# Interaction stage of a four-layer graph network: the order of VectorE's step, the add of a pair's sums moved to third place

## The reference

```
p1    = tanh(h @ pp_W1 + pp_b1) @ pp_W2 + pp_b2
inter = concat(p1[src], p1[dst]) @ pi_W1 + pi_b1
inter = (inter @ pi_W2 + pi_b2) @ pi_W3            # E x (64*8)
i1    = einsum('ecb,eb->ec', inter.reshape(E, 64, 8), edge_attr_8)
i1    = tanh(i1 @ ii_W1 + ii_b1) @ ii_W2 + ii_b2
out   = segment_sum(i1, dst)
```

## Time and profile before

| | before |
|---|---|
| median of 3 runs | 10613.77 us (10609.83 to 10619.3) |
| profiled execution | 10609.71 us, span 10608.1 us |
| PE, DVE, ACT, POOL busy | 56%, 41%, 23%, 65% of the span |
| gathers of the interaction stage | 1664, first start 4054.9 us, last 6334.5 us |

### The profile page before, as it was taken

How to read it: one execution, slowest core, us unless ns; L and a number is a source line. 1 busy time by engine, 2 the same in 40 slices (tenths; PEclk the granted TensorE clock), 3 DMA queues, 4 the chain that set the end, 5 groups by cost and what they waited for, 6 DMA issues and landing times.

```text
span 10608.1 us, 144590 instructions
## 1 busy us (share of the span) xinstructions
PE 5928.7 (56%) x31865; PEld 3642.0 (34%) x32026; DVE 4356.3 (41%) x11981; ACT 2422.2 (23%) x4618; POOL 6911.9 (65%) x7936
## 2 busy tenths in 40 slices
PE   6999997344444447888888882343333322222222
PEld 4777773222222223333333331232223211111111
DVE  5888884222322224666666662111111111111111
ACT  4999992000000002333333330000000000000000
POOL 2333330577777776766666666777777767777777
PEclk9999995555555558999999995555555555555555
DMA  3333332111111112222222221111111111111111
GB/s 96 97 97 97 97 96 79 48 29 30 29 30 29 30 30 48 57 56 56 56 56 56 56 51 23 28 28 28 28 28 28 28 24 28 28 28 28 28 28 27
DMA packets 503888, 488.54 MB, mean 46 GB/s; under 512 B 245340, under 2 KB 299425, under 8 KB 503777
## 3 DMA queue, kind: packets, MB, share of 16 engines
q0 software_dynamic: 220480, 235.58, 11.8%
q1 hardware_dynamic: 283360, 252.43, 8.2%
HBM read 427.04 MB, written 61.15 MB: 46 GB/s over the span
## 4 chain that ended last, share of the span: by engine, by line
POOL 43%; PE 25%; issue 19%; DVE 8%; DVEq 2%; POOLq 1%; ACT 1%; DMA 0%; another core or an unknown queue 0%; ACTq 0%; SPq 0%
POOL mov L668 43%; PE ps L1524 5%; PE ps L1413 4%; PE ps L1387 3%; PE ps L1420 3%; DVE scr L937 3%; PE ps L1516 2%; PE ps L1449 2%; PE ps L1543 1%; DVE sel L927 1%; PE ps L1411 1%; PE ps L1534 1%; DVE acc L946 1%; PE ps L1427 1%; PE ps L1428 0%
## 5 line engine op out<-in xcount | busy, mean ns | idle before, releaser
L1387 PE MATMUL ps<-outs,mov 128*64 128x64 f32 x9984 | 1371.0, 319 | 4210.3 <-DMA mov<-tab_q,idx 1613.2
L1387 PEld LDWEIGHTS ps<-outs,mov 128*64 128x64 f32 x9984 | 1158.7, 222 | 4538.9 <-issue 4538.9
L837 DVE TENSOR_TENSOR acc<-acc,ps 64x64 f32 (+1 forms) x1664 | 353.6, 213 | 4432.5 <-PE ps L1387 4430.3
L668 POOL DMA_INDIRECT outs<-tab_u,idx x1664 | 1595.7, 959 | 735.8 <-issue 472.5
L668 POOL DMA_INDIRECT mov<-tab_msg,idx x1664 | 1575.4, 947 | 759.6 <-issue 492.2
L668 POOL DMA_INDIRECT mov<-tab_h,idx x1664 | 1570.2, 944 | 576.2 <-issue 506.5
L668 POOL DMA_INDIRECT mov<-tab_q,idx x1664 | 1570.2, 944 | 543.8 <-issue 506.5
L937 DVE TENSOR_TENSOR scr<-ps,scr 128x512 f32<-128x512 f32 x1664 | 1050.8, 682 | 266.7 <-PE ps L1516 184.2
L1524 PE MATMUL ps<-scr,w_bas 128*64 128x512 f32 x3328 | 899.9, 619 | 0.0
L631 POOL TENSOR_TENSOR scr<-outs 128x128 f32<-128x128 f32 x416 | 191.8, 461 | 834.9 <-DVE outs L847 834.0
L847 DVE TENSOR_TENSOR outs<-rel,iota_w 128x256 f32<-128x256 f32 x1664 | 705.4, 424 | 43.3 <-issue 30.2
(11 more groups left out here) (215 smaller groups left out, 8602.6 us busy)
## 6 DMA issues: line engine op xcount, KB each, us to landing
mov<-in_dst_row SPq DMA_DIRECT2D x832, 128.0 KB, 2.7
mov<-in_ea_T SPq DMA_DIRECT2D x416, 128.0 KB, 2.5
tab_msg<-outs SPq DMA_DIRECT2D x104, 256.0 KB, 2.0
mov<-tab_msg,idx POOLq DMA_INDIRECT x1664
outs<-tab_u,idx POOLq DMA_INDIRECT x1664
mov<-tab_h,idx POOLq DMA_INDIRECT x1664
mov<-tab_q,idx POOLq DMA_INDIRECT x1664
win<-tab_g SPq DMA_DIRECT2D x416, 32.0 KB, 2.4
```

Source lines behind the costliest of these rows:

```text
L668: nc.gpsimd.indirect_dma_start(out=gat(e, u)[:, k, :], out_offset=None, in_=table, in_offset=bass.IndirectOffsetOnAxis(ap=idx[:, u, k:k + ...
L837: nc.vector.tensor_tensor(into, into, bank(banks[u % len(banks)])[0:rows, 0:W], ALU.add) \
L1387: last = mm(bank(banks[u % len(banks)])[0:width, 0:W], values(u)[:, k, :], sel(e, u)[:, k, :], start=k == 0, stop=k == TL - 1)
```

## The change

In VectorE's list for the interaction stage the add of pair n-7 goes from the first place to behind `sel_pair`; the index copy, products 0 and 1, `selT_pair` and `sel_pair` come ahead of it. Nothing else is changed: the lags, the buffers, the semaphores and the other engines' lists stay.

```
-                return [(7, add_pair), (0, idx_pair), (4, z_stage(0)), (4, z_stage(1)), (2, selT_pair), (5, sel_pair), (4, z_stage(2)),
+                return [(0, idx_pair), (4, z_stage(0)), (4, z_stage(1)), (2, selT_pair), (5, sel_pair), (7, add_pair), (4, z_stage(2)),
                         (4, z_stage(3)), (4, z_stage(4)), (4, z_stage(5)), (4, z_stage(6)), (4, z_stage(7))]
```

## The result

The changed kernel takes 10457.4 us (median of 4 runs, 10455.4 to 10458.9) against 10614.4 (4 runs, 10609.8 to 10619.3) for the kernel before: a ratio of 0.9852, 95% interval 0.9835 to 0.9869, 157 us less. Forecast were 10456 and 158 less. The profiled execution has a span of 10455.0 us. (The title's "third place" is loose: in VectorE's list of twelve entries the add went from the first to the sixth.)

A forecast was written before the change was run, and what follows sets the result against it. Bound: PE and VectorE taking turns in the interaction stage, POOL held back. 45 turns from 44.5 to 41.3 us give 144, first turns 17; 161, rounded to 158: median 10456 us, range 10430 to 10545 (forecast's own 10435 to 10490).

The forecast's parts named there:

- The ring between PE and VectorE: Interaction stage: PE's sum, VectorE's add, copy and products, then PE's spreads take turns, 44.5 us per four pairs; POOL held back.
- The ordinary step: One pair without norm or turn opening, between PE's window loads: falls from 10.73 to 9.5 us, chained from PE's unwaited distances.
- Add and selections hidden by the window and identity matmuls: Behind PE's sum: the add's 0.59 and sel's 0.67 us cost nothing, since product 2 waits for its spread anyway.
- The norm step: Step with a node group's layer norm before VectorE's first entry: stays 12.04 us, same instructions in another order.
- the opening: Step opening a turn of four pairs, where VectorE reads eight starts: 0.3 us charged for that, 0.5 for projection, 10.3 in all.
- The first turns: First seven turns of the stage, bound by gathers: 10.05 us a pair against 10.73, some 17 us gained.
- The sum: 45 turns from 44.5 to 41.3 us give 144, first turns 17: together 161 us, rounded down to 158.
- The port: Index copy and selT beside gathers: whole-instruction blocks would cost 40 us of the gain (10496); longest block seen 0.17 us.
- half a gain: First rival: VectorE still late to product 2, opening costs its full 1.2 us; about 10539; 0.23 together with the second rival.
- POOL's own gap of 0.9: Second rival: the gap at each pair's start isn't from a late index; 42.7 us per turn, 10516; 0.23 with the first.
- sel waits for the same sum anyway: Third rival, no gain: VectorE stays serial and product 2 comes no earlier; 10614 us; chance 0.04.
- lengthened gathers: Fourth rival, slower: VectorE's earlier instructions lengthen all gathers, 44.7 us per turn, 10624 or more; chance 0.03.

The follow-up runs named there:

- experiment 2: Kernel before with products 0 and 1 alone moved ahead of the add, index copy, selT and sel staying behind it: 10452.1 us, ratio 0.9851.
- the fillers: Changed kernel with one or three extra compares of sel's size behind the add, results unused: 10479.2 us with one, 10602.9 us with three.
- experiment 11: Changed kernel with three of four gathers per chunk in the interaction stage: 10437.0 us, against 10457.4 with four.
- experiment 4: Changed kernel with three extra compares of sel's size behind the add, results unused: 10602.9 us, ratio 0.9993 to the kernel before.
- run 944: Not a run's label: 944 is the median gather time in ns of every other run, against 947 in the change's.
- experiment 10: Changed kernel with its layer norm cut and spread evenly over the steps, and three of four gathers per chunk: 10334.8 us, against 10416.7 with four.
- experiment 1: Kernel before with the index copy alone moved ahead of the add; products, selT and sel stay behind the sum: 10574.5 us, ratio 0.9966.

## Why the prediction was right

**The ring between PE and VectorE as the bound, POOL held back by it.** Right, and shown from both sides: the index copy alone gives 36 us, fewer gathers give 12 on before, and products 0 and 1 alone give the whole 157.

**The ordinary step, 10.73 to 9.5.** Measured 9.42. A turn of before has two ordinary steps, though, 10.23 and 10.73, and the chain starts from the longer; since the gain was summed from whole turns, nothing hangs on that. The chain of unwaited distances held row by row but for one: from spread 4 to the weigh behind it I took 0.64, and it is 0.54 (5168.09 to 5168.63).

**Add and selections hidden by the window and identity matmuls.** Right: product 2 waits for its spread, even with 1.9 us behind the sum (experiment 2), and the fillers priced the slack at about what was worked out. One sign came out only in part: sel was to wait 0.5 to 1 us for the sum. From 4600 to 6100 us it waits 36 times in 146 pairs, at most 0.8; in the step shown the two short instructions of the residual update have taken up that time, and sel starts unwaited 0.43 after the window load.

**The norm step keeps 12.04, the opening takes 10.3.** Measured 12.10 and 10.22 in the turn shown, 12.18 and 10.23 on average: the norm step grew by 0.17 instead of staying, and at the opening VectorE's delay is 10.22 - 9.42 - 0.45 = 0.35, for which 0.3 was charged. A turn came to 41.25, against the 41.3 of the sum. So the sum took the norm step too short and the other three steps slightly too long, and the two partly cancel. Why the norm step grew isn't shown.

**The first turns, bound by gathers.** POOL's pace there, 10.08 us per pair (1.260 x 8) for 10.05 forecast, says little, since it was the same before: POOL then ran ahead into free buffers. PE's window loads decide: 10.23 us per step over the first 28 instead of 10.78, 15.5 us less where 17 were forecast. With fewer gathers (experiment 11) these steps go down to 9.54, so the gathers did bound them.

**The sum.** 161 had been added up, and the stage by itself gained 161. The rounding to 158 had another reason, that POOL's and PE's bounds would sometimes meet, and nothing shows that they did. The median gained 157. That forecast and median meet within 1 us is luck; that they meet within some 5 us isn't.

**The clock.** The reading of the page was slightly off: slice 16 shows 7 for PE and 8 for the clock, since it begins before the stage. From 4300 us on the granted clock is 1.00, before (to 6340) and after (to 6180), so PE's durations could be used as they are.

**POOL's idle time.** Forecast 357 us before 1080 gathers; 379.3 / 1174 x 1080 = 349.

**The port.** It cost nothing here, but not for want of blocks. The prediction took 0.17 us as the longest block on either side, from selT and the gathers, and left out the index copy: in the trace of before that takes up to 0.42 us, with a median of 0.17. After the change 133 of 205 index copies start inside a gather, where it was 117. Yet fewer were lengthened, 39 copies (50 before) and 133 gathers (256 before). The longest block of the change is 0.26 us, on a gather (1.205 less 0.947). Neither kind reached the path in ordinary steps.
When a block comes can be read from the traces. An index copy that starts 0.1 to 0.5 us into a gather isn't lengthened (none of 18 before, none of 49 after); one that starts 0.52 to 0.76 into it ends with the gather (49 of 49, 29 of 30). So does the copy shown above, 5163.19 + 0.38, with its gather, 5162.62 + 0.95:

```profile
5162.62 0.95 POOL L668 DMA_INDIRECT outs<-tab_u,idx  x1 [0.30 <-issue]
```

The whole-instruction block of the Trainium skill ("SBUF — State Buffer", "Who interferes with whom") would have cost 40 us that didn't come: the copy waited for the last part of a gather at most. In the other direction a gather did wait for three compares in a row, by nearly a microsecond (experiment 4). The same section infers that descriptor generation isn't held up by a compare with both inputs in SBUF; these gathers, which read their indices from SBUF, were. Whether the reading of the indices is the reason isn't shown.

The rivals: half a gain fell with the spacing of the ordinary steps; POOL's own gap of 0.9 fell with 0.30 at 186 of the 208 pair openings; "sel waits for the same sum anyway" is true of sel and beside the point, since the products it stood behind had left; lengthened gathers stayed at a mean of 956 ns, far below the 1.09 us from which they decide. That gathers can pass it locally is shown by experiment 4.

What isn't settled: the change took 5 us more than experiment 2, and the runs of the two don't overlap (10455.4 to 10458.9, 10450.9 to 10453.7), although its stage is the one that is 4 us shorter. In the profiled executions the other three gather stages account for it, 9 us longer together in the change's; its gathers have a median of 947 ns, those of every other run 944. The kernel before was 4 us longer beside the change as well, and the ratios are equal. Why that group ran slower is open. Open too is why three compares cost 1.5 us in the norm step (experiment 4).

## What to carry to other kernels

In an engine that runs a hand-written list in order, put behind a wait for another engine's last work only what needs that work; whatever can already run goes ahead of it, and then the other engine has its input when it comes round. Chain the other engine's distances where it shows no wait: that gives the new step, and the slack left for what now stands behind the wait. And ask what bounds next before estimating the gain: here three more limits lay within 6 us of a turn of 44.5: VectorE's norm at 41.25, the gathers at 40.3, and PE with VectorE at 39.05 (experiment 10). Each needed its own edit.

## What the runs showed of the hardware

- A wait that is removed can come back under another name: index copies on time took 101.2 us of "DVE idx" idle from POOL, and its "PE" idle rose from 56.8 to 114.4 us (experiment 1), for 36 us of time.
- After a late index copy the next gather starts 0.88 to 0.95 us later (166 pair openings of the kernel before); with the copy done in time it starts 0.30 after the one before it. A late release costs about 0.6 more than its lateness.
- Three compares with both inputs in SBUF, back to back, stretched a gather issued with them from 0.94 to 1.90 us: all 143 gathers that started beside them ended 0.82 to 0.83 us after the last compare (experiment 4). In the change, with two such compares in a row, no gather of the stage was stretched by more than 0.26.
- An index copy on VectorE (0.17 us) beside a gather is held only in the gather's last part: started 0.52 to 0.76 us into it, it ends with the gather; started 0.1 to 0.5 into it, it isn't held (before and after).
- VectorE's sequencer needs 1.84 us for eight values read from SBUF, and an index copy behind it waits (by 1.56 at the opening of the turn shown); six small dependent instructions next to it raised the opening step from 10.2 to 12.2 us.
